# A graph kernel's pair stage: ranks as maxima read straight from PSUM

## The reference, cut to what matters

```python
def _sage(x, src, dst, Wn, bn, Wr):
    msg = x[src]
    agg = jax.ops.segment_sum(msg, dst, num_segments=N)
    deg = jax.ops.segment_sum(jnp.ones((src.shape[0],), x.dtype), dst, num_segments=N)
    mean = agg / jnp.maximum(deg, 1.0)[:, None]
    return mean @ Wn + bn + x @ Wr
h = jax.nn.relu(_sage(x, src, dst, W1n, b1n, W1r) + (x @ Wl1 + bl1))
out = _sage(h, src, dst, W2n, b2n, W2r) + (h @ Wl2 + bl2)
x = _layernorm(x + out)
```

## Time and profile before

| | us |
|---|---|
| median of 3 runs | 3968.42 (3966.04 to 3969.57) |
| the profiled execution | 3963.56 |
| its span | 3961.8 |
| pair stage, first step's start to the last full step's end | 1214.3 |
| usual step in it | 24.69 |
| DVE busy in the span | 3283.6 |
| PE busy in the span | 3079.3 |
| ACT busy in the span | 2245.2 |

### The profile page before, as it was taken

One profiled execution on the slowest core, in us unless ns is written; L12 is line 12 of the kernel. 1 busy time (PEld: TensorE's weight loads), 2 busy tenths in 40 slices (PEclk: granted clock), 3 DMA queues, 4 the chain that ended last, 5 costly groups with the idle time before them and its releaser, 6 DMA issues.

```text
span 3961.8 us, 125753 instructions
## 1 busy us (share of the span) xinstructions
PE 3079.3 (78%) x50473; PEld 2741.7 (69%) x50473; DVE 3283.6 (83%) x6987; ACT 2245.2 (57%) x5930; POOL 1372.6 (35%) x1644
## 2 busy tenths in 40 slices
PE   0288888888888859999777777777766888788786
PEld 0176667776677759899677777777755777777775
DVE  7599999999999933233699999999976989889897
ACT  5334444444444320000587888787855888888887
POOL 2000000000000000000287787787762555555554
PEclk9999999999999989999899998998986888878886
DMA  8156666666666679899677777777737888888884
GB/s 208 54 166 201 203 202 198 193 189 203 204 195 193 201 266 375 348 337 331 221 248 228 238 244 230 224 253 230 234 121 239 258 250 260 256 259 255 249 255 142
DMA packets 655940, 907.66 MB, mean 229 GB/s; under 512 B 363977, under 2 KB 587882, under 8 KB 636411
## 3 DMA queue, kind: packets, MB, share of 16 engines
q1 hardware_dynamic: 633240, 800.64, 63.1%
q10 hardware_dynamic: 19763, 94.38, 6.3%
q0 software_dynamic: 2352, 4.52, 0.5%
HBM read 651.96 MB, written 247.40 MB: 227 GB/s over the span
## 4 chain that ended last, share of the span: by engine, by line
DVE 35%; PE 34%; DMA 10%; ACT 9%; issue 8%; SPq 2%; POOL 1%; ACTq 1%; DVEq 0%; POOLq 0%
PE ps L639 7%; PE ps L979 7%; DVE U L769 4%; DMA U<-AD 4%; PE ps L664 3%; DVE U L1286 3%; DVE EDG L1315 3%; DMA T<-ROWS 3%; DMA A<-ROWS 2%; DVE U L1278 2%; PE ps L1193 2%; DVE U L1647 2%; ACT U L553 2%; DVE EDG L1652 2%; PE ps L1205 2%
## 5 line engine op out<-in xcount | busy, mean ns | idle before, releaser
L553 ACT ACTIVATE U<-ps 128x512 bf16<-128x512 f32 (+1 forms) x637 | 356.1, 576 | 493.0 <-PE ps L651 492.9
L1163 POOL TENSOR_TENSOR EDG<-U,edge 128x256 f32<-128x256 f32 x343 | 242.2, 706 | 848.8 <-DVE edge L1311 733.9
L1479 ACT ACTIVATE U<-U,T 128x65 f32<-128x65 f32 x1806 | 459.8, 339 | 108.7 <-PE ps L1567 96.9
L490 POOL DMA_INDIRECT U<-REC,nod x49 | 70.7, 1443 | 1190.3 <-PE ps L595 1068.0
L1193 PE MATMUL ps<-U 128*128 128x65 bf16 x7203 | 299.8, 198 | 214.0 <-DVE edge L1289 211.8
L979 PE MATMUL ps<-U 128*128 128x192 bf16 x4802 | 416.6, 247 | 37.6 <-DVE U L1056 21.3
L979 PEld LDWEIGHTS ps<-U 128*128 128x128 bf16 x4802 | 401.4, 98 | 46.3 <-DMA U<-AD 21.8
L792 DVE TENSOR_TENSOR EDG<-edge,EDG 128x896 bf16<-128x896 bf16 x686 | 411.0, 619 | 20.1 <-issue 11.9
L1193 PEld LDWEIGHTS ps<-U 128*128 128x128 bf16 x7203 | 261.1, 101 | 237.7 <-DVE edge L1289 234.9
L1505 POOL TENSOR_TENSOR U<-U 128x455 f32<-128x455 f32 x258 | 276.6, 1072 | 329.7 <-DVE U L1647 329.7
L664 PE MATMUL ps<-EDG,U 128*128 128x193 bf16 x2401 | 319.1, 256 | 76.8 <-ACT U L553 61.1
(11 more groups left out here) (305 smaller groups left out, 7585.7 us busy)
## 6 DMA issues: line engine op xcount, KB each, us to landing
U<-AD SPq DMA_DIRECT2D x98, 1568.0 KB, 8.5
U<-ROWS SPq DMA_DIRECT2D x343, 448.0 KB, 4.4
OND<-EDG SPq DMA_DIRECT2D x343, 224.0 KB
OSD<-EDG SPq DMA_DIRECT2D x343, 224.0 KB
AD<-U ACTq DMA_DIRECT2D x49, 1568.0 KB, 6.3
EDG<-ROWS SPq DMA_DIRECT2D x343, 224.0 KB, 5.0
U<-OND SPq DMA_DIRECT2D x303, 224.0 KB, 5.2
EDG<-OSD SPq DMA_DIRECT2D x189, 224.0 KB, 4.7
```

The costliest lines, as they stand in the source:

```text
L553: ev4.by(act.activation(prow[i % NPW][:, P * g:P * (g + m)], ps[4 + gg % 2][:, 0:P * m], ACT.Copy))
L1479: ins = act.activation(V4[k % NV][:, 0, c, :], H[d % 3][:, s, :], ACT.Copy, scale=a4[d % 2][:, s:s + 1])
```

## The change

The triangle gets 256 on its diagonal, and `offb` is lowered by 256 (a bias in ACT's copy L569). In a row of `OH` the edge's own source block is the only one that meets the diagonal, so its running number comes out as before, and that of every other block 256 lower, below zero. The maximum over the 49 numbers is then the edge's own without a mask. So the copies to `RUN`, the product `PRD` and both pairs of buffers go, and DVE takes the maxima straight from `ps[0]` and `ps[1]`, in two instructions a half. PE's next half waits for `rank_ok` from DVE in place of `run_ev` from ACT. PE's second half moves from n = 4 to n = 5, DVE's first ranks from n = 4 to n = 3.

```diff
-            dv.by(dve.tensor_copy(triub[:, :], triup))
+            dv.by(dve.scalar_tensor_tensor(triub[:, :], ident[:, :], 256.0, triup, ALU.mult, ALU.add))
+            dv.by(dve.memset(sc[:, 40:41], -256.0))
...
-            def runs(j, h):
-                act.wait_ge(run_mm.at, 2 * j + h + 1)
-                k = 2 * j + h
-                if k >= 2:
-                    act.wait_ge(rank_ok.at, k - 1)
-                act.activation(RUN[h][:, 0:5, :, :].rearrange("p c i k -> p (c i k)"), ps[0][:, 0:490], ACT.Copy)
-                run_ev.by(act.activation(RUN[h][:, 5:9, :, :].rearrange("p c i k -> p (c i k)"), ps[1][:, 0:392], ACT.Copy))
...
-                        off_ev.by(act.activation(offb, ps[2][0:CP, 256:256 + NB], ACT.Copy))
-                    if j is not None and n in (1, 4):
-                        runs(j, (1, 4).index(n))
+                        off_ev.by(act.activation(offb, ps[2][0:CP, 256:256 + NB], ACT.Identity, bias=sc[0:CP, 40:41]))
...
                 if k:
-                    pe.wait_ge(run_ev.at, k)
+                    pe.wait_ge(rank_ok.at, k)
...
-                        elif n in (1, 4):
-                            runs(j, (1, 4).index(n))
+                        elif n in (1, 5):
+                            runs(j, (1, 5).index(n))
...
             def ranks(j, h):
-                k = 2 * j + h
-                dve.wait_ge(run_ev.at, k + 1)
-                if k >= 2:
-                    dve.wait_ge(rank_ok.at, k - 1)
-                dv.by(dve.tensor_tensor(PRD[h], OH[j % 2][:, HC * h:HC * h + HC, :, :], RUN[h], ALU.mult))
-                own()
-                rank_ok.by(dve.tensor_reduce(RK[:, j, HC * h:HC * h + HC, :], PRD[h].rearrange("p c i k -> p c k i"), AX, ALU.max))
+                dve.wait_ge(run_mm.at, 2 * j + h + 1)
+                for b, (c0, c1) in enumerate(((0, 5), (5, 9))):
+                    ins = dve.tensor_reduce(RK[:, j, HC * h + c0:HC * h + c1, :],
+                                            ps[b][:, 0:2 * NB * (c1 - c0)].rearrange("p (c i k) -> p c k i", i=NB, k=2), AX, ALU.max)
+                rank_ok.by(ins)
...
-                        elif n in (4, 8):
-                            ranks(j, (4, 8).index(n))
+                        elif n in (3, 8):
+                            ranks(j, (3, 8).index(n))
```

More of the change, by code:

```diff
@@ L423, in gnn_kernel @@
         HC = CP // 2
[L424 to L427, removed]
         OHR = [part(o2 + 1152 * i, 1152).bitcast(BF16).rearrange("p (c r k) -> p c r k", c=HC, k=2) for i in range(2)]
@@ L457, in gnn_kernel @@
         rec_t, rec_ev = sem("rec_turned"), sem("rec_evac")
-        src_hot, off_mm, off_ev, run_mm, run_ev = sem("src_hot"), sem("off_mm"), sem("off_evac"), sem("run_mm"), sem("run_evac")
+        src_hot, off_mm, off_ev, run_mm = sem("src_hot"), sem("off_mm"), sem("off_evac"), sem("run_mm")
         rank_ok, fld_hot, slot_mm, slot_ev, slot_ea = sem("rank_ok"), sem("field_hot"), sem("slot_mm"), sem("slot_evac"), sem("slot_evac_act")
```

## The result

| | before | after |
|---|---|---|
| median us | 3967.45 (4 runs) | 3911.32 (3907.67 to 3914.72, 4 runs) |
| profiled execution, us (span) | 3963.56 (3961.8) | 3914.72 (3913.0) |
| a usual step, us | 24.69 | 23.97 |
| steps over 26 us, of the 44 from the fifth start to the last | 12 | 0 |

The ratio is 0.9858, with a 95% interval of 0.9841 to 0.9875: 56 us faster. The forecast was 3928, inside a range of 3905 to 3950.

What follows compares the result with a forecast made beforehand. DVE was taken to bound the pair stage, PE close behind. Steps of 37 x 23.91 + 8 x 26.4 = 1095.9 us against 1132.9, with 4 us from the first steps, save 41 us: 3928 us, range 3905 to 3950.

Steps and rivals of the forecast that it cites:

- The new chain: In a usual step of the pair stage, PE's transpose through to the X update sets the length: 23.91 us, 0.78 less.
- the gap of DVE: Before the X update in a usual step, DVE waits some 0.65 us instead of 0.19.
- PE's new wait: Before PE's transpose, which DVE's scaling releases behind the first ranks, PE waits 0.8 us.
- its arrival at the count: PE can count at 20.31 us into the step, DVE's comparison is done at 19.87; PE later by 0.4 us.
- The price of the reductions: DVE's two reductions from PSUM cost 1.06 us a half, saving 0.58 us a half and 1.15 us a step.
- The bias: ACT's offsets' copy takes 0.09 us longer with a bias, and PE's first runs end later by as much.
- the number of low-clock steps: Of 45 pair-stage steps, 8 at 26.4 us with TensorE's clock low, between 3 and 12; 12 before the change.
- The rival that the clock falls in most steps: PE's new wait makes TensorE's clock fall in each step, 45 x 26.4 us, giving 4019 us; chance 0.08.
- The "before" of the sum: The forecast's total for the 45 full pair-stage steps of the unchanged kernel, 1132.9 us.
- The first steps: Steps 0 to 3 of the pair stage, with little PE work, save 4 us in all, bounds 0 and 6.
- ACT's busy time: ACT loses its four copies a step, so its busy time in the pair stage is 105 us lower.
- Behind the stage: The 2598 us that follow the pair stage have no change.

Runs made afterwards that it cites:

- scale_first: The changed kernel with DVE's scaling, which releases PE's transpose, put ahead of the first ranks and the two field products; 3889.67 us, ratio 0.9798.
- x_later: The changed kernel with the X update one comparison later on DVE and nothing else; 3891.66 us, ratio 0.9803.
- dup_first: The changed kernel with one unused reduction of 490 elements added ahead of the first half's ranks; 3965.38 us, ratio 1.0001.
- dup_second: The changed kernel with one unused reduction of 490 elements added ahead of the second half's ranks; 3917.17 us, ratio 0.9868.
- direct_only: The changed kernel, ranks straight from PSUM, but with both placements (PE's second runs, DVE's first ranks) as before; 4060.41 us, ratio 1.0234.
- order_only: The kernel before with only the two moves (second runs to n = 5, first ranks to n = 3), masks and ACT's copies kept; 4031.39 us, ratio 1.0148.
- the first two groups of experiments: The runs that take the change apart into its halves, and those that test the chain that sets the step by moved or added instructions.
- before_fill_second: The kernel before with an extra reduction of 490 elements from SBUF on DVE ahead of the second half's ranks; 3988.68 us, ratio 1.0051.

## Why the prediction was right, and where it was off

**The new chain** (scaling, transpose, second runs, slots, counts, ACT, X update) was right and close in size: 23.91 forecast, 23.97 measured; the gap of DVE 0.65 and 0.63; PE's new wait 0.8 and 0.66; its arrival at the count later than DVE's comparison. From the start of the step at 446.01 the links stand where they were forecast: transpose 11.22 (11.23), second runs 11.39 (11.34), slots 12.93 (12.88), the count behind the slots 20.38 (20.31), X update 21.55 (21.49). scale_first, x_later, dup_first and dup_second show that it is this chain, and neither DVE's sum nor PE's work. The 0.14 us of difference at PE's wait is a matter of counting: the trace counts idle time from the end of the last use (456.06 and 0.52), where the forecast had let it take 0.35 us, the distance from start to start. The count ahead of it waits for DVE's comparison at the time forecast (8.95 and 8.96), so the longer wait for the offsets' copy, 0.39 us against 0.29 before, delays nothing there.

**The price of the reductions** was right: 1.06 us a half forecast, 1.05 measured, durations 659 and 555 ns. Without its elements each costs about 147 to 149 ns, as L785 with 350 ns for 192 does (150). The Trainium skill's 62 cycles more for a read from PSUM ("VectorE: DVE Perf Modes", the TRN2 errata) do not show: the trace does not agree. As an estimate from that page's figure, the pair would have taken 1.18 us.

**The bias** was right: the offsets' copy went from 203 to 295 ns.

**The term that was mis-sized is the number of low-clock steps.** I took 8, at 2.5 us; there are 0. That is 20 us, and it is all of the difference between 3928 and 3911 and a little more; the usual step, 0.06 us longer than forecast in 45 steps, and the first steps took back 5. The midpoint between 3 and 12 had no reason behind it other than that strings of long steps might not form. That there is none was not forecast, and no run shows why: the 21 us that the 12 long steps gave back, over a third of the gain, were luck as far as the forecast goes, which had counted on 4 fewer of them, not 12. The rival that the clock falls in most steps was wrong for this kernel, but not idle: direct_only and order_only, each one half of this change, show it with 44 and 20 long steps, with a longer PE wait at the place that it named. Whether the narrow offset matmuls ahead of it have a part in this, no run tests. Its price for all steps, 55 us on the time before, was too low for direct_only by 37 (4060 against 3968 and 55). The "before" of the sum, 1132.9 us, is 0.7 too high: 33 steps of 24.69 and 12 of 26.45 are 1132.2.

**The first steps** were a smaller miss. From the first L743 to the fifth it was 81.43 us and is 79.74: 1.7 us, not 4. The first ranks still wait for PE (4.86 us before the first, 2.81 before the next).

**ACT's busy time** fell by 81 us, not 105: the two copies of a half overlap by a tenth of a microsecond (in the trace before, starts at 463.67 and 464.15, the first of 0.58 us). If each of the 196 overlaps a neighbour so, that is about 20 us, and the bias took 4.5 back.

**Behind the stage** I had forecast no change. The pair stage ends 55.6 us earlier in the profiles (read at DVE's next reciprocal behind it, 1432.7 before, 1377.1 after), the execution 48.8. Over the ten profiles of the first two groups of experiments and of the two kernels, the part behind the stage lasts between 2526 and 2539 us with no order by edit, so these 7 us are scatter of single executions; the medians differ by 56.

## What to carry to other kernels

A saving counts for what is queued behind it on the chain that sets the loop: the same 0.59 us of VectorE was worth 0.57 us ahead of the instruction that releases PE, and 0.12 us behind it. When a reader moves from SBUF to the PSUM bank itself, the bank's next writer waits for that reader, so the two have to be placed anew together: each half of this change alone was 1.5 to 2.3% slower. After such a change, look for the new wait and put the instruction that releases it first; here that, and moving one late-released instruction behind its neighbour, gave another 28 us. And count the steps of low clock as a term of their own: they moved by 12 here without a forecast for it.

## What the runs showed of the hardware that I had not expected

A wait of PE of 1.99 us in each step, between a use and the second runs, went with the lower level of the clock (0.50, 1.2 GHz) in all of 44 steps, one of 1.40 us before the transpose in 20 of them and one of 1.23 us in 13. Waits of 0.66 and 0.9 us at the same place did not. Behind a wait of 1.8 us before a count it was 22 of 44, behind one of 1.27 us there 7 (the last of them ahead of a step that is no longer among the 44). In the kernel before it was 12, behind waits of 0.30 and 0.50 us, so these sizes are no rule. Each time the clock stayed low for 6.8 or 3.4 us of matmuls with hardly a gap (PE busy for 2.00 of 2.00 us in direct_only). For direct_only this made 4060 us of an expected 3960; for before_fill_second, where DVE sets the step, most of it was hidden.
